# A fused transformer block on one core: the first tile's queries and keys are turned after the sixteenth projection instead of in front of the fifteenth

## What is computed

```
qkv = layernorm(x) @ qkv_w + qkv_b            # 2048 rows, 128 -> 384
q = q / (norm per head of 8) * qn_scale + qn_bias      # k likewise
theta = {gate, val, proj}
loss = mean((swish(k @ gate) * (k @ val)) @ proj - v)^2)
for _ in range(2):                            # two training steps
    theta = theta - 0.1 * newton_schulz(grad(loss)(theta))
```

## Time and profile before

| | |
|---|---|
| time, median of 3 runs | 819.97 us (819.3 to 822.01) |
| the profiled execution | 819.79 us, its span 818.0 us |
| TensorE busy | 753.3 us, 92% of the span |
| VectorE busy | 519.8 us, 64% |
| ScalarE busy | 382.7 us, 47% |
| GpSimd busy | 266.6 us, 33% |
| front and start of the pipeline | 0 to 47.2 us of the span |

### The profile page before, as it was taken

How to read it: one execution, slowest core, us unless ns; L and a number is a source line. 1 busy time by engine, 2 the same in 40 slices (tenths; PEclk the granted TensorE clock), 3 DMA queues, 4 the chain that set the end, 5 groups by cost and what they waited for, 6 DMA issues and landing times. The chain is left out here.

```text
span 818.0 us, 15239 instructions
## 1 busy us (share of the span) xinstructions
PE 753.3 (92%) x5432; PEld 601.2 (73%) x5432; DVE 519.8 (64%) x1570; ACT 382.7 (47%) x1080; POOL 266.6 (33%) x465
## 2 busy tenths in 40 slices
PE   5699999979999989888599999999999999999786
PEld 2389999859998878786357667777777777778764
DVE  5755555455555544457877777766766776664477
ACT  4533333543332362213457666655666655663224
POOL 5691000068000011004624444433334333442027
PEclk9799999999999999958889999999999999999679
DMA  8000000000000000000000000000000000000001
GB/s 249 4 0 2 1 1 1 2 0 2 1 1 1 2 1 1 1 1 0 1 1 2 1 2 1 2 2 2 2 2 1 2 1 2 1 2 2 1 0 52
DMA packets 9464, 7.15 MB, mean 9 GB/s; under 512 B 1584, under 2 KB 9008, under 8 KB 9264
## 3 DMA queue, kind: packets, MB, share of 16 engines
q1 hardware_dynamic: 9392, 6.19, 2.5%
HBM read 5.14 MB, written 1.05 MB: 8 GB/s over the span
## 5 line engine op out<-in xcount | busy, mean ns | idle before, releaser
L1324 POOL TENSOR_SCALAR t_p_<-t_p_,t_rinv_ 128x128 f32<-128x128 f32 (+3 forms) x256 | 132.5, 535 | 202.4 <-DVE t_rinv_ L1520 202.4
L1354 ACT ACTIVATE t_p_<-t_p_,t_nmin_ 128x128 f32<-128x128 f32 (+3 forms) x256 | 140.0, 551 | 9.6 <-DVE t_nmin_ L1513 9.6
L1513 DVE CUSTOM_DVE_ANT_0 t_p_<-t_S_,t_mask_ 128x128 f32<-128x128 f32 (+3 forms) x256 | 112.9, 488 | 21.6 <-PE t_S_ L1411 17.3
L1359 ACT ACTIVATE t_pT_<-t_T_ 128x384 f32<-128x384 f32 (+1 forms) x96 | 50.6, 527 | 118.2 <-PE t_T_ L1423 118.2
L1423 PEld LDWEIGHTS t_T_<-ident,t_p_ 128*128 128x128 f32 x640 | 68.2, 141 | 45.0 <-issue 26.1
L1411 PE MATMUL t_S_<-t_k_,t_q_ 64*128 64x256 f32 (+3 forms) x512 | 95.0, 468 | 0.1
L1423 PE MATMUL t_T_<-ident,t_p_ 128*128 128x128 f32 x640 | 90.8, 281 | 0.3 <-ACT t_pT_ L1359 0.3
L1438 PEld LDWEIGHTS t_O_<-t_pT_,t_v_ 128*64 128x64 f32 x1280 | 69.2, 137 | 11.0 <-ACT t_pT_ L1359 10.5
L1438 PE MATMUL t_O_<-t_pT_,t_v_ 128*64 128x128 f32 x1280 | 76.9, 275 | 0.0
L717 POOL TENSOR_TENSOR gvl<-gv,gvh 128x512 fp32r<-128x512 f32 x2 | 2.5, 1274 | 204.3 <-ACT gvh L824 204.3
L1411 PEld LDWEIGHTS t_S_<-t_k_,t_q_ 64*128 64x128 f32 x512 | 41.4, 185 | 26.9 <-DVE t_nmin_ L1513 12.3
(11 more groups left out here) (254 smaller groups left out, 1707.3 us busy)
## 6 DMA issues: line engine op xcount, KB each, us to landing
wqkv<-in_L_attn_b_w_qkv_dram SPq DMA_DIRECT2D x1, 1536.0 KB
x<-in_L_attn_a_x_dram SPq DMA_DIRECT2D x4, 256.0 KB, 3.9
out_dram<-x SPq DMA_DIRECT2D x4, 256.0 KB, 2.3
we<-in_L_ffn_We_dram SPq DMA_DIRECT2D x1, 512.0 KB
wout<-in_L_attn_b_w_out_dram SPq DMA_DIRECT2D x1, 512.0 KB
gv<-n_L_attn_a_ttt_gate_dram SPq DMA_DIRECT2D x1, 256.0 KB, 4.8
gv<-in_L_attn_a_ttt_val_dram SPq DMA_DIRECT2D x1, 256.0 KB, 6.0
proj<-n_L_attn_a_ttt_proj_dram SPq DMA_DIRECT2D x1, 256.0 KB, 4.7
```

The costliest lines, as they stand in the source:

```text
L1324: last = pool.tensor_scalar(pr[:, G.par, h, cols], pr[:, G.par, h, cols], rinv[:, G.par, n:n + 1], 1.0, ALU.mult, ALU.mult)
L1354: act.activation(pr[:, G.par, h, cols], pr[:, G.par, h, cols], ACT.Exp, bias=nmin[:, G.par, n:n + 1], scale=-1.0, accum_out=rsum[:, G.par, ...
L1359: act.activation(pT[:, G.par, 0, G.blocks], psT[:, 0, 0:G.width], ACT.Copy).then_inc(t["eA"], 1)
L1513: dve.tensor_tensor_reduce(pr[:, G.par, h, cols], psS[:, (2 * G.n + h) % 3, at_:at_ + keys], mask[:, SEQ - keys:SEQ], 1.0, -NEG, ALU.add, ...
```

## The change

In `Front.tensor` the call of `turn_first()` moves from step 14 (`NT - 2`) to behind the loop, after the projection of tile 15. In `Front.scalar` `take_first()` moves from step 15 to step 16, and in `Front.vector` from step 16 to step 17. No instruction is added or removed, no buffer changes, and no transfer moves.

```diff
@@ Front.scalar
-            if s == NT - 1:
+            if s == NT:
                 take_first()
@@ Front.tensor
                 last.then_inc(self.s["pt"], 1)
-            if s == NT - 2:
-                turn_first()
+        turn_first()
@@ Front.vector
-            if s == NT:
+            if s == NT + 1:
                 take_first()
```

## The result

Measured first were nine executions of each kernel: 814.18 us in the median for the changed one (813.21 to 817.54), 819.97 for before (816.82 to 823.8), ratio 0.9935 with a 95% interval of 0.9916 to 0.9955. Both kernels were measured again in four later batches; a batch is a set of executions taken together on one chip. All 45 executions of the changed kernel average 817.1 us, and the 158 of before from the later batches 819.5, which makes 2.4 us, with an interval of 1.5 to 3.4 if every execution counts as independent. Without the first nine, which raised the question, the 36 later ones average 817.6, and the difference is 1.8 us (0.8 to 2.9). So the first comparison showed more than twice the difference that stays.

The account below looks back on a forecast made before the run. TensorE was taken to bound the kernel from 47.2 us, with VectorE's chain and the idle time at GpSimd's result setting the pipeline's start. Terms -1.33 - 0.37 + 0.1 = -1.6 us gave 818.3 us, range 815.9 to 821.0.

Parts of the forecast that it names:

- The order's share: Front's end on TensorE: tile 14's projection no longer stands behind the wait for GpSimd and starts 1.33 us sooner.
- that projection's clock: Tile 14's projection ends before the clock falls to half, taking 0.88 us in place of 1.25: 0.37 us gained.
- The bias of tile 14: On VectorE, in the front's end: starts at 28.30 us in place of 29.99, 1.70 us sooner.
- First forward: TensorE's first forward matmul, waiting for VectorE's low part: starts near 32.1 us in place of 33.43, 1.3 us sooner.
- Second forward: TensorE's forward of the second tile: starts at 37.6 us in place of 39.30, 1.70 us sooner.
- The two terms of the sum: Gains at the front's end: 1.33 us from idle time and order, 0.37 us from the clock under one projection.
- Costs put at nothing: Front's end: the later turn is covered, tanh has 0.2 us slack, and GpSimd's square of tile 12 doesn't show.
- The clock's return in the front: Full clock returns near 42.6 us; the cost lies between 0 and 0.3 us, taken as 0.1.
- the rival of the kept clock: Clock holds or returns before the second forward: 1.34 us more gained at the second tile, 816.8 us; chance 0.20.
- the late clock: Clock returns past 46 to 48 us: 819.8 to 821.3 us up to about 51, slower beyond; chance 0.15.
- no later stage waits for a clock time: Behind the front: TensorE has no slack, so whatever the front's chain gains is handed on.
- The clock's part: Rivals at the front: clock kept, 816.8 us, chance 0.20; clock back late, 819.8 us or more, chance 0.15.

Follow-up runs that it names:

- e1: The kernel before, unchanged, timed again against itself; median 818.23 us, ratio 0.9997.
- e5: The kernel before with two useless ScalarE copies in front of the first copy of the second Newton-Schulz phase; median 818.84 us, ratio 1.0001.
- e9: The kernel before with one useless ScalarE copy in front of the first copy of the first Newton-Schulz phase; median 818.9 us, ratio 0.9997.
- e6: The changed kernel with six useless ScalarE copies in front of the first copy of the second Newton-Schulz phase; median 821.44 us, ratio 1.0032.
- e10: The changed kernel with one useless ScalarE copy in front of the first copy of the first Newton-Schulz phase; median 817.6 us, ratio 0.9976.
- e11: The changed kernel with sixteen matmuls of zeros in front of the first gram matmul of the first Newton-Schulz phase; median 822.17 us, ratio 1.0031.
- e2: The changed kernel, unchanged, timed again beside the kernel before; median 815.63 us, ratio 0.9957.
- e3: The changed kernel with VectorE's part undone, the low part in front of the sum of tile 14 again; median 816.38 us, ratio 0.9956.
- e4: The kernel before with only TensorE's turn moved one step, behind tile 14's projection and in front of tile 15's; median 816.32 us, ratio 0.997.
- e13: The changed kernel, unchanged, timed once more; median 816.91 us, ratio 0.9971.
- e14: The changed kernel, unchanged, timed again for a second independent trace; median 819.67 us, ratio 0.9988.
- e7: The changed kernel with ten matmuls of zeros between the turn of the first queries and keys and the first forward; median 815.68 us, ratio 0.9959.

## Why the prediction was wrong, and where it was right

*The order's share was right.* The prediction had tile 14's projection 1.33 us sooner; it is 1.30 (2.20 less 0.90). It had 0.37 us more from that projection's clock: 0.91 us for 1.25 makes 0.34. The bias of tile 14 was to come 1.70 us sooner, and does so by 1.64 (28.97 for 29.99, less the later start of 0.62). First forward 1.3 us sooner: 1.32. Second forward 1.7: 1.63, and 11.17 in all four traces of the changed kernel, while the three of before have 12.36, 12.70 and 12.80. So before averages 12.62, and the mean gain up to there is 1.45. The two terms of the sum are cut a little differently than in the prediction: with no early fall of the clock the gain is 1.19 us (e1), where the wait counted 1.33, and an early fall costs up to 0.44 more in these traces (12.80 less 12.36), where 0.37 was put, and only in executions that have it. e5 and e9, whose front is that of before, have 13.30 and 12.37; e6, e10 and e11, with the new front, 11.17 or 11.18.

*Costs put at nothing were nothing.* The later turn of the first queries and keys was covered, and tanh didn't wait for TensorE: it stands behind the end of its table load, at 34.66 us. GpSimd's square of tile 12, done at 29.45, did not hold up VectorE, whose sum of it starts at 29.48.

*The clock's return in the front had the wrong sign.* From second to third forward the traces of before take 7.89, 7.75 and 8.00 us, those of the changed kernel 7.38, 6.58, 7.73 and 7.74, in the mean 0.5 us less, where the prediction had put 0.1 us of cost. In e2 the clock was back at 37.6 us, before the second forward at 39.64: that is the rival of the kept clock, priced at 1.34 us, and it has 6.58 us where before averages 7.88. With the 1.45 that makes 2.0 us for the front. One slip stands in the late clock: a return at 51 us makes 822.3 by its own 0.5 us for each microsecond, so "819.8 to 821.3" stops short.

*The step that failed* is the sentence that "no later stage waits for a clock time", with the range that was built on it, whose lower edge of 815.9 us the measured 814.18 passes. I let the granted clock vary only between 28.9 and 51 us. In the first pair of profiles 3.3 of the 4.8 us lie behind 298 us, and in two executions of the one changed kernel the same instructions behind it take 3.1 us more or less (458.82 and 461.89), with shorter or longer stretches at half clock. In before's profile these lie at 305 to 309 us, 370 to 377 us and 401 to 415 us; the changed kernel's first profile lacks the first and has 3.4 us in place of 6.9 and 10.3 in place of 13.8 of the others. The clock's part was named as a rival but priced at the front alone, and the profile of before was taken for what every execution does. Its later stages were of the long kind, with much time at half clock, and all nine executions of the changed kernel in the first comparison were of the short kind, as far as their mean granted clock shows it (0.955 to 0.961). Of the 36 later ones 17 have a clock under 0.9535 and average 820.3 us; the other 28 of the 45 average 815.1. In before 77 of 158 are under it (821.1), the others average 818.0. The line at 0.9535 was drawn afterwards and is rough: e10's trace has 0.955 and the fall near 305 us, e3's 0.953 and no fall. With both kinds in, the difference is 2.4 us or 0.3%, where the first medians differ by 5.8.

*What stays open.* The forecast's 1.6 us is inside what all executions say (1.5 to 3.4), and so are the 2.0 of the front's traces. Whether the change also makes the short kind more frequent (62% against 51%) can't be said: by batch, the changed kernel had 0 of 9, 2 of 12 and 15 of 24 executions of the long kind. That is more uneven than independent draws would make likely, so executions of one batch seem to share something, and the interval above is then too narrow. Batch by batch the mean difference was 5.9, 3.3 and 1.2 us. What it is that they share was not tried. The chip is one candidate, since the two later batches with the changed kernel ran on different ones; before itself averages 819.2 to 819.8 us in the four later batches, and on the chip that served two batches the fall near 305 us is in one of four traces and then in three of three. Nor do the runs show what decides in an execution whether that fall comes.

## What to carry to other kernels

In a list that runs in order, a job that waits for the slowest chain should stand behind everything that is ready: here one turn in front of a projection cost 1.2 us with the clock kept through the projections and 1.6 us in the first profile, and moving it by one place (e4) brought the same distance as the whole edit. When a small change moves later stages that it doesn't touch, compare the same stretch of the program between fixed landmarks in several traces of each kernel before believing it. The profile of one execution gave the length of the chain to 0.01 us where the clock fell behind the projections (11.17 in the new order, 12.36 and 12.37 in the old), and to 0.9 us where it could fall under them (12.36 to 13.30 in the old). For a kernel whose clock falls in its gaps it doesn't give the time of the kernel to 3 us, and neither do nine executions.

## What the hardware showed that I had not expected

One and the same kernel has a fall of TensorE's clock near 305 us in some executions and not in others (e2 without, e13 and e14 with it), and the fall makes the stretch around it 1.63 us longer. 2.2 us more of added work cost 5.1 us (e11 against e10). The executions of an unchanged kernel spread over 10 us (815.5 to 826.0 in before). And holding the clock with useless matmuls in one gap (e7) won nothing: the clock then fell behind the next gap, 11.9 us behind tile 13's projection, where the first fall came after 5.3 to 6.5 us in the changed kernel.

The Trainium skill says (TensorE: Matmul & The Clock Gate, "What's actually happening") that what grants the clock doesn't restart with a kernel. The traces agree: in the four of the changed kernel, which all have a distance of 11.17 us, the first fall of the front comes 6.54, 5.53, 5.27 and 5.36 us behind tile 13's projection, and in before's three 2.44, 6.53 and 2.54 us.
